# The second norm's result turned in 32x32 blocks by VectorE and moved by DMA, the low-rank part one step later

## What is computed

```
x = _layernorm(x + attn(x, wq, wk, wv, wo))        # 32 heads of 32, grouped keys, causal
x = _layernorm(x + xattn(x, ctx, weight))          # three-tap convolution over the sequence's rows
x = _layernorm(x + ffn(x, A, B, Wr, br))

ffn:    router_logits = x @ Wr.T + br              # 8 experts
        scores = 8 * softmax(router_logits)
        low = x @ A.T                              # 8 experts of rank 16: 128 values a row
        out = 2 * sum over experts and rank of low * scores * B
```

## Time and profile before

| | us |
|---|---|
| runs, median (lowest to highest) | 1471.19 (1468.21 to 1471.94) |
| profiled execution, its own time | 1470.48 |
| its span, first to last instruction | 1468.6 |
| first stage, to about | 816 |
| second stage, steady steps | 850 to 1426 |
| tail of the second stage | 1427 to 1468.6 |

### The profile page before, as it was taken

The page is one execution under the profiler, slowest core; times in us unless marked ns, Lnnn a source line. Parts: engine busy times, 40 slices in busy tenths (PEclk is TensorE's granted clock), DMA queues, the critical chain, the costliest instruction groups (busy, mean ns, idle before and its releaser), DMA issues. The chain is left out here.

```text
span 1468.6 us, 32393 instructions
## 1 busy us (share of the span) xinstructions
PE 1368.0 (93%) x8288; PEld 1058.0 (72%) x8288; DVE 1092.8 (74%) x3965; ACT 930.5 (63%) x3258; POOL 984.2 (67%) x936
## 2 busy tenths in 40 slices
PE   6899999999999999999996699999999999999994
PEld 4667676676676676766764488888888888888873
DVE  5767777777777677777776468877888888778875
ACT  5777777787878777777877255545555555545543
POOL 3667676667667676666666377777777777777763
PEclk9999999999999999999998799999999999999997
DMA  6345444444445344444447767667766666767651
GB/s 224 113 117 147 120 139 130 123 143 116 142 116 143 116 144 119 139 130 123 145 138 208 186 158 159 161 162 170 168 150 159 163 165 156 160 164 171 156 116 44
DMA packets 108861, 213.03 MB, mean 145 GB/s; under 512 B 26640, under 2 KB 32272, under 8 KB 108816
## 3 DMA queue, kind: packets, MB, share of 16 engines
q1 hardware_dynamic: 108816, 212.51, 54.1%
HBM read 131.83 MB, written 34.47 MB: 113 GB/s over the span
## 5 line engine op out<-in xcount | busy, mean ns | idle before, releaser
L432 PE MATMUL wo_ps<-weights,halves 128*128 128x512 f32 x2304 | 572.5, 399 | 12.1 <-DVE weights L610 12.0
L432 PEld LDWEIGHTS wo_ps<-weights,halves 128*128 128x128 f32 x2304 | 422.6, 189 | 129.5 <-issue 34.4
L693 ACT ACTIVATE pexp<-sm,smin 128x128 f32<-128x128 f32 x1024 | 398.3, 392 | 175.9 <-DVE smin L561 175.8
L1040 PE MATMUL wo_ps<-weights,halves 128*128 128x512 f32 x1488 | 400.6, 402 | 2.0 <-DVE yz L1143 2.0
L812 POOL TENSOR_TENSOR pn<-pexp,prec 128x512 f32<-128x512 f32 x256 | 268.8, 1050 | 196.2 <-DVE prec L568 196.2
L1393 POOL TENSOR_TENSOR prods<-prod,prods 128x512 fp32r<-128x512 f32 x192 | 260.3, 1364 | 133.8 <-ACT prods L1287 128.9
L1040 PEld LDWEIGHTS wo_ps<-weights,halves 128*128 128x128 f32 x1488 | 273.0, 190 | 61.0 <-issue 3.7
L561 DVE CUSTOM_DVE_ANT_0 sm<-s_ps,mask_t 128x128 f32<-128x128 f32 x1024 | 231.9, 282 | 67.0 <-PE s_ps L462 62.3
L1287 ACT CAST prods<-prod 128x512 fp32r<-128x512 f32 x192 | 118.8, 621 | 165.8 <-DVE prod L1177 129.3
L1177 DVE TENSOR_TENSOR prod<-att,x 128x512 f32<-128x512 f32 x192 | 186.1, 985 | 13.9 <-DMA att<-sim_scratch 11.1
L693 ACT ACTIVATION_READ_ACCUMULATOR pexp<-sm,smin 128x1 f32 x1024 | 193.5, 189 | 0.0
(11 more groups left out here) (99 smaller groups left out, 1661.1 us busy)
## 6 DMA issues: line engine op xcount, KB each, us to landing
att<-sim_scratch SPq DMA_DIRECT2D x192, 252.0 KB
pt<-blocks SPq DMA_DIRECT2D x640, 64.0 KB, 2.0
ctx_t<-in_ctx SPq DMA_DIRECT2D x32, 576.0 KB, 4.7
raw<-in_xT SPq DMA_DIRECT2D x32, 512.0 KB, 3.6
raw<-ot_scratch SPq DMA_DIRECT2D x32, 512.0 KB, 6.8
xn<-in_x SPq DMA_DIRECT2D x32, 512.0 KB, 7.5
out<-late SPq DMA_DIRECT2D x32, 512.0 KB, 6.3
ot_scratch<-ot SPq DMA_DIRECT2D x63, 256.0 KB, 2.1
```

What stands on the lines that cost most here:

```text
L432: mm = pe.matmul(qkv_ps[(par + g) % 2][:], xs[:, par, xl, k], w_sb[:, wl, g, k], start=(k == 0 and n == 0), stop=(k == KT - 1 and n == 2))
L693: ins = nc.scalar.activation(pexp[:, c % 2, i * P:(i + 1) * P], sm[:, c % 2, i * P:(i + 1) * P], ACT.Exp, bias=smin[:, c % 2, i:i + 1], sc ...
L1040: mm = pe.matmul(wo_ps[n][:], os_t[:, par, ol, k], wo_sb[:, wl, k, n * BANK:(n + 1) * BANK], start=(k == 0 and m == 0), stop=(k == KT - 1 ...
```

## The change

x2 is no longer turned by PE, except for the last two tokens (30 and 31, whose work lies in the tail). Instead DVE turns it in 32x32 blocks with one instruction (`block_x2`) into a new tile `blocks`, whose layout is [partition, block of rows, row, k], so that its writes lie KT = 8 numbers apart. SP then moves the 4x4 blocks with sixteen DMAs (`move_x2`), each 32 partitions by 256 numbers (32 KB), into `xt`, whose layout is now [partition, row, k]: `reduce_rank` reads its stationary operand `xt[:, :, k]` with a step of 8 numbers. `reduce_rank`, `route`, `gates` and `gate_low` now work on token z = t-3, one step later than before, and `turn_low`, `low_lt` and `expand` follow in the same step. The store of the output is one step later too. `prods` and `lt` move into the place of weights no longer used.

```
     def later_weights(weights):
...
+            hi[:, rest:rest + PB * 2 * BANK].rearrange("p (m l n) -> p m l n", m=PB, l=2),
+            lo[:, rest + 2 * TAPS * P:rest + 2 * TAPS * P + 2 * S].rearrange("p (l s) -> p l s", l=2))
...
-    xt = sb("xt", [P, KT, S])
+    blocks = sb("x2_blocks", [P, QB, SB, KT])
+    xt = sb("xt", [P, S, KT])
...
-    LAST = B + 2
-    LEAD, TAIL = 6, 5
+    LAST = B + 3
+    LEAD, TAIL = 6, 6
+    MOVES = 16 * QB * QB
...
+        def move_x2(t):
+            wait(sp, low_done, after(t - 1, 1, 1))
+            wait(sp, x2_blocked, after(t, 1, 1))
+            for b in range(QB):
+                for q in range(QB):
+                    sp.dma_start(xt[q * SB:(q + 1) * SB, b * SB:(b + 1) * SB], blocks[b * SB:(b + 1) * SB, q]
+                                 ).then_inc(xt_in, 16)
...
+            if valid(t - 4):
+                wait(sp, normed[2], after(t - 4, 1, 1))
+                sp.dma_start(out[t - 4], res[:, par]).then_inc(stored[par], 16)
             if valid(t) and not at_step(t, 0):
                 load_att(t, 0)
-            if valid(t - 3):
-                wait(sp, normed[2], after(t - 3, 1, 1))
-                sp.dma_start(out[t - 3], res[:, 1 - par]).then_inc(stored[1 - par], 16)
+            if valid(t - 2) and not at_step(t, B) and not at_step(t, B + 1):
+                move_x2(t - 2)
             if valid(t) and not at_step(t, 0):
                 load_att(t, 1)
...
         def reduce_rank(t):
-            wait(pe, xt_in, after(t, 2, 2))
+            if at_step(t, 0):
+                pe.wait_ge(consts_in, 48)
+            if at_step(t, B - 2) or at_step(t, B - 1):
+                pe.wait_ge(xt_copied, 2 * (t - B + 3))
+            else:
+                wait(pe, xt_in, after(t, MOVES, MOVES))
+                wait(pe, added[2], after(t - 1, 2, 1))
             for k in range(KT):
-                mm = pe.matmul(ffn_place(t)[0][:, 0:LOWW], xt[:, k], wa_t[:, k * LOWW:(k + 1) * LOWW],
+                mm = pe.matmul(ffn_place(t)[0][:, 0:LOWW], xt[:, :, k], wa_t[:, k * LOWW:(k + 1) * LOWW],
                                start=(k == 0), stop=(k == KT - 1))
             mm.then_inc(low_done, 1)
...
                 if valid(z):
-                    if s == 1:
+                    if s == 3:
+                        reduce_rank(z)
+                    if s == 10:
                         turn_low(z)
-                    if s == 3:
+                    if s == 13:
                         expand(z)
-                if valid(f):
-                    if s in (11, 12):
-                        turn_x2(f, par, s - 11)
-                    if s == 14:
-                        reduce_rank(f)
...
         convolve(B - 2, 4)
-        turn_low(B - 3)
+        reduce_rank(B - 3)
         convolve(B - 2, 5)
-        expand(B - 3)
...
+        def block_x2(t, par):
+            wait(dve, normed[1], after(t, 1, 1))
+            wait(dve, xt_in, after(t, MOVES, 0))
+            dve.transpose(blocks[:].rearrange("p q s k -> p q k s"),
+                          x2[:, par].rearrange("p (k q d) -> p q k d", k=KT, q=QB)).then_inc(x2_blocked, 1)
```

More of the change, by code:

```diff
@@ L100, in later_weights @@
 def later_weights(weights):
-    lo = weights[:, NG * KT * BANK:2 * NG * KT * BANK]
+    hi, lo = (weights[:, part * NG * KT * BANK:(part + 1) * NG * KT * BANK] for part in range(2))
     both = weights[:].rearrange("p (l m) -> p l m", l=2)
@@ L1055, in turn_x2 @@
         def turn_x2(t, par, n):
-            if at_step(t, 0) and n == 0:
-                pe.wait_ge(consts_in, 48)
-            wait(pe, normed[1], after(t, 1, 1))
-            if at_step(t, B - 2):
+            pe.wait_ge(normed[1], t + 1)
+            if t == B - 2:
                 pe.wait_ge(added[0], 2 * (B - 1) + n + 1)
             else:
-                last = t - 2 if at_step(t, B - 1) else t - 1
-                wait(pe, added[2], after(last, 2, n + 1))
+                pe.wait_ge(added[2], 2 * (t - 2) + n + 1)
             for k in range(NJ):
@@ L1078, in turn_low @@
             wait(pe, gated_done, after(t, 1, 1))
+            if not at_step(t, B - 2) and not at_step(t, B - 1):
+                wait(pe, added[2], after(t - 1, 2, 2))
             pe.transpose(ffn_place(t)[1][:, 0:S], gated[:], id_t[:]).then_inc(low_turned, 1)
@@ L1218, in step @@
                 average(f, 1)
+            if valid(z):
+                route(z)
             if valid(c):
                 multiply(c, 1 - par, 1)
+            if valid(z):
+                gate_low(z)
+            if valid(c):
+                multiply(c, 1 - par, 2)
+            if valid(t):
+                add(t, par, 0, 0)
+                count(t, 0, 0)
+            if valid(z):
+                low_lt(z)
+            if valid(f):
+                block_x2(f, par)
+            if valid(c):
+                multiply(c, 1 - par, 3)
+                multiply(c, 1 - par, 4)
+            if valid(z):
+                add(z, 1 - par, 2, 0)
+                add(z, 1 - par, 2, 1)
+            if valid(c):
+                add(c, 1 - par, 1, 0)
+                count(c, 1, 0)
             if valid(z):
@@ L1225, in step @@
             if valid(c):
[L1226 to L1237 removed]
                 multiply(c, 1 - par, 5)
[L1239 to L1242 removed]
+        steps(dve, step, 0, B - 1, LEAD, TAIL - 4)
         def finish(t):
@@ L1257, in _ @@
         average(B - 2, 1)
-        for m in range(PB):
-            multiply(B - 1, 1, m)
+        multiply(B - 1, 1, 0)
+        route(B - 3)
+        multiply(B - 1, 1, 1)
+        gate_low(B - 3)
+        multiply(B - 1, 1, 2)
+        low_lt(B - 3)
+        multiply(B - 1, 1, 3)
         finish(B - 3)
-        for m in range(PB, UNITS):
-            multiply(B - 1, 1, m)
+        multiply(B - 1, 1, 4)
+        multiply(B - 1, 1, 5)
         add(B - 1, 1, 1, 0)
@@ L1297, in normalise2 @@
             wait(act, shifted[1], after(t, 1, 1))
+            wait(act, added[2], after(t - 2, 2, 2))
             nc.scalar.activation(x2[:, par], yz[:, 1], ACT.Identity, bias=shift[1][:],
@@ L1301, in copy_x2 @@
         def copy_x2(t, n):
[L1302 to L1305 removed]
+            act.wait_ge(x2_turned, 2 * (t - B + 2) + n + 1)
+            act.wait_ge(low_done, t)
+            nc.scalar.copy(xt[:, :, n * NJ:(n + 1) * NJ].rearrange("p s k -> p k s"),
+                           ffn_place(t)[n][:].rearrange("p (k s) -> p k s", k=NJ)).then_inc(xt_copied, 1)
         def gates(t):
@@ L1340, in step @@
             if valid(z):
-                normalise3(z, 1 - par)
-            if valid(f):
-                copy_x2(f, 0)
-            if valid(c):
-                high_prod(c, 3)
-            if valid(f):
-                copy_x2(f, 1)
-            if valid(c):
-                high_prod(c, 4)
-            if valid(f):
-                gates(f)
-            if valid(c):
-                high_prod(c, 5)
-        steps(act, step, 0, B - 1, LEAD, TAIL - 3)
+                high_lt(z)
+            if valid(c):
+                for m in range(PB, UNITS):
+                    high_prod(c, m)
+            if valid(z):
+                normalise3(z, 1 - par)
+        steps(act, step, 0, B - 1, LEAD, TAIL - 4)
+        normalise1(B - 1, 1)
+        high_prod(B - 1, 0)
+        gates(B - 3)
+        high_prod(B - 1, 1)
+        normalise2(B - 2, 0)
         high_lt(B - 3)
-        normalise1(B - 1, 1)
-        normalise2(B - 2, 0)
-        for m in range(UNITS):
+        for m in range(2, UNITS):
             high_prod(B - 1, m)
@@ L1420, in step @@
             if valid(c):
-                for m in range(3, UNITS):
-                    low_prod(c, m)
-        steps(pool, step, 0, B - 1, LEAD, TAIL - 3)
+                low_prod(c, 3)
+                low_prod(c, 4)
+            if valid(z):
+                invert_root(z, 2)
+            if valid(c):
+                low_prod(c, 5)
+        steps(pool, step, 0, B - 1, LEAD, TAIL - 4)
         invert_root(B - 1, 0)
```

51 lines of the change are left out of this document (15 added, 36 removed).

## The result

| | before | after |
|---|---|---|
| runs, median (lowest to highest), us | 1471.42 (1468.21 to 1471.94) | 1660.08 (1658.57 to 1661.06) |
| profiled execution, its own time | 1470.48 | 1659.12 |
| its span | 1468.6 | 1657.3 |
| mean granted TensorE clock | 0.982 | 0.936 |

The changed kernel takes 1.1286 times as long, interval [1.1267, 1.1306]. The forecast was 1567, with a range to 1655: the direction is right, the size is not. The measured time lies outside the range, 5 us above its end.

A forecast was written before the change was run, and what follows sets the result against it. PE was taken to bound the kernel at 19.48 us a step; the change makes a longer loop through DVE and SP's moves. Start 866.1, 28 rounds of 22.6, 15.8, then tail 41.8 + 8.4 give span 1564.9, time 1567, range 1505 to 1655.

The forecast's parts named there:

- The rounds: Low-rank product to low-rank product, 28 times: chain through PE, DVE and SP of 22.2 us, plus 0.4 for clock, 22.6.
- what follows from token 28's product on: End of kernel: 15.8 us left of step 31, then the tail's 41.8 plus 8.4 for the last tokens' later work.
- The bound, the moved wait and the moves: PE would idle 3.6 us a round before the low-rank product, awaiting sixteen SP moves of 11.35 us to last landing.
- DVE's part of the chain without the turn: Second norm, router and gate, third product, next token's statistics and half of lt on DVE; 7.42 us including a turn of 1.38.
- DVE's own round: DVE's work of 18.0 us a step plus a 2.2 us hole before the first product: 20.2, above the present 19.48.
- The block turn: DVE's new turn of 1024 numbers a partition: 1.38 us, twice the row for 512; low end 1.2, high end 2.8.
- The product: PE's low-rank product reading xt, priced at its present 1.85 us in the round.
- rival B: Strided access doubles the block turn (1.4 more) and low-rank product (1.85 more): round 25.4, time 1652; chance 0.23.
- The clock term: PE behind its new pause: lower clock could add 2.4 us a round; 0.4 was charged.
- One in six: Assumed share of PE's new pauses followed by the lower clock, giving 0.4 us a round.
- Rival A: DVE's own round of 20.2 us binds if moves are issued faster, from 0.49 apart: time 1500; chance 0.14.
- Rival C: PE stays the bound and time falls by 26 us to 1445, needing moves landed within 7.8 us; chance 0.05.

The follow-up runs named there:

- the kernel that doesn't wait: Changed kernel with doubled xt, its low-rank product using moves issued a step earlier, and read and write unstepped: 1464.99 us, 0.9963 of the kernel before.
- wide moves: Changed kernel with eight moves of 512 numbers a partition instead of sixteen of 256, both accesses still stepped: 1503.73 us, 1.0228 of the kernel before.
- pause filled: Changed kernel with read and write unstepped, plus twelve unused matmuls just ahead of the low-rank product: 1559.03 us, against 1602.91 without them.
- the last kernel: Changed kernel with k ahead of the row in both tiles, SP issuing eleven moves and ACT five, behind its high halves of products 3 and 4: 1497.55 us.
- short runs on two queues: Changed kernel with k ahead of the row in both tiles (128-byte runs), SP issuing eleven moves and ACT five ahead of its high halves: 1501.35 us.

## Why the forecast was right in its mechanism and wrong in its size

From 1564.9 to 1657.3 the span is 92.4 off. The rounds carry 28 x (25.53 - 22.6) = 82; the first product is at 866.01 (866.1 forecast), and what follows from token 28's product on takes 76.4 instead of 66.0. Three products in its chain of waits, 4.2, 4.2 and 3.7 where 1.85 stood, are 6.6 of these 10.4; the rest was not taken apart.

The 2.93 that a round is too long by can be split with the stepped product's 4.09 behind a wait at full clock: the product + 2.24, the block turn + 0.83, the clock + 0.16, DVE's other work - 0.31, together 2.92. Over 28 rounds that is 63 + 23 + 4 - 9 = 81 of the 82. **The step that failed is the price of the two stepped accesses, above all 1.85 for the product.**

- **The bound, the moved wait and the moves: right.** The sixteen moves take 15 x 0.634 + 1.88 = 11.39 from first issue to last landing; forecast 11.35. PE waits for them in every round, DVE for ACT 2.3 and for the convolution piece. Line 306's ten moves were the right row for moves of half the size. (Their 6.23 us span nine distances and one issue, so that the row says 0.627 rather than 0.623.)
- **DVE's part of the chain without the turn: 0.3 too long.** From the convolution piece to the turn it is 5.73, forecast 7.42 - 1.38 = 6.04. The third product takes 0.69, not 0.9: the product's mean fell to 706 ns from 985. In the steady part before, 72 of 124 products ran for most of their time beside an instruction of POOL of over 0.9 us and took 1.25 us in the mean, and those with little or none beside them 0.68; in after none ran so. The two go together; no experiment changed that alone. DVE's own round, put at 20.2, is 18.93, of which 1.1 comes from cheaper products: one takes 831 ns in the mean of 1000 to 1400 in the kernel that doesn't wait, against 1009 before, six times a round.
- **The block turn: mis-sized.** 1.38 forecast, 2.21 measured, + 0.83 a round or 23 us. The unstepped turn takes 1.23; the stepped write was the part that no row of before showed, and I took the value nearest to the row without a step. The bound of 2.8 held it.
- **The product: failed, and it is the largest miss.** 1.85 forecast. The stepped read makes it 3.70 at full clock (wide moves, no wait), which was rival B's value, and 4.09 at full clock behind a wait. In after it is 4.10 to 4.23, always behind a wait. Of the + 2.24, 1.97 is the step and 0.27 the start behind a wait, which the plain product shows too (2.12 for 1.85).
- **The clock term: wrong in its reasoning, near in its size by luck.** "One in six" should have been all. PE's part of the chain, product, projection and convolution piece, takes 5.5 and 6.6 in turn, mean 6.04. At full clock the same three take 4.09 + 0.69 + 0.70 = 5.48 behind a wait in the kernel with wide moves, so the clock costs 0.56 a round where 0.4 was forecast. It is so little only because the stepped read leaves the product nothing to lose: with both accesses unstepped, as the forecast priced them, the clock costs 1.45 (pause filled against not), and the forecast would have been 28 x 1.05 = 29 us short by it. I had one pause of 4.30 with the clock low behind it, and gave the new pause of 3.6 a sixth of that by its shorter length. Pauses of 3.4 were already followed by the low clock in nearly all rounds.
- **Rival B: right in its mechanism.** Its price for the product came true (3.70), that for the turn about half (+ 0.83 for + 1.4), and its round, 25.4, is 0.1 short of the measured 25.53, its time, 1652, 8 us. That it came so near is in part luck: it charged too much for the turn, and nothing for the clock and for the start behind a wait. The Trainium skill (Advanced Engine Details and Errata, section SBUF Cachelines) has the penalty for accesses that each touch another line, and the runs agree: 1.23 to 2.21 for DVE's write, 1.85 to 3.70 for PE's weight read. The page's rule spoke for B and I gave B 0.23.
- **Rival A** (DVE binds) is excluded for after by DVE's waits. It became true only in the kernel that doesn't wait for its moves. **Rival C** (PE stays the bound) is excluded; it needed the moves off the chain, and then the time is 1465 to 1505, not 1445, since DVE or the stepped read takes over.

The forecast's own arithmetic is tested by the kernel with both accesses unstepped and the pause filled: 1559.03 measured against 1564.9 + 1.9 - 28 x 0.4 = 1556 without the clock term. So the structure of the sum stands. What failed are the prices of the two operations whose stepped access no row showed: both were put in as if the step were free, and both lie in the one chain that sets the round.

What stays open: why the rounds of the last kernel differ among themselves (19.1 to 22.3). The clock accounts for some of the long ones. Its moves also land later in some, and no run tells whether the other transfers or the short runs are the reason.

## What to carry to other kernels

A change that takes work off the bound engine but sends its input round three others makes a new loop: sum that loop, with every DMA issue in it at the issuing engine's pitch (0.63 us each here, whatever the bytes), and compare it with the bound engine's own work. If the loop is longer, the bound engine pauses once a round. Behind pauses of TensorE of 3.4 us and more, once a round, the clock fell in nearly every round here; so charge it in each, but only to operations that nothing else holds up already. And where the new layout makes an engine step 32 bytes between float32 numbers, take twice the unstepped time for it until a run shows otherwise.

## What the runs showed of the hardware

- Stepping 32 bytes costs nearly the factor of two on both sides: DVE's block turn of 1024 numbers takes 2.21 instead of 1.23 when its write steps, PE's sixteen float32 matmuls of 136 columns 3.70 instead of 1.85 when the weight read steps, both at full clock. The mean weight load is 334 ns against 190.
- A product whose weight read steps hardly feels the clock. After has two in its tail that PE doesn't wait for; its timeline, and the windows in them:

```profile
1631.87 3.89 PE L1090 MATMUL wo_ps<-wa_t,xt 128*128 128x136 f32 x16
1640.14 3.87 PE L1090 MATMUL ffn_ps<-wa_t,xt 128*128 128x136 f32 x16
```

```profile
1634.00:1635.00 1.00, 1.00 (x6) 1.00 (x6) 0.15 (x2) 0.00 (x0) 0.69 (x2) 0.50 0.00 0
1641.00:1642.00 1.00, 1.00 (x6) 1.00 (x5) 0.97 (x3) 0.00 (x0) 0.00 (x0) 1.00 0.00 0
```

  3.89 with most of it at half the clock and 3.87 at the full one; behind a wait 4.22 and 4.09. The plain product goes from 2.12 to 3.99 behind a wait. The four times fit two limits of which the larger one counts, so that taking away either alone brings little.
- Pauses of 3.4 to 4.4 us of PE once a round were followed by a granted clock of 0.50 in nearly every round, pauses of 0.75 in none; in the last kernel, with pauses of 0.5 to 2.7 in front of the product, the clock was low in it in four of 28 rounds. Twelve needless matmuls in the pause brought 44 us.
- Moves from SBUF to SBUF in runs of 128 bytes are little dearer than in runs of 1 KB: landing 2.0 instead of 1.9, pitch 0.66 instead of 0.633, 20 us in all. The Trainium skill (DMA: Bandwidth & Descriptors, section Why small descriptors are slow (HBM only)) says that transfers within SBUF don't pay for small descriptors, and for the landing on one queue the trace agrees. It doesn't for the DMA engines' own time: a packet of 128 bytes took 14 ns in the mean and one of 1 KB 62 to 65, so the same bytes keep the engines busy 1.7 times as long. With short runs on two queues the DMA share is 0.89 and the median landing of SP's moves 3.8 instead of 2.0.
- ACT issues a DMA in about the time that SP does (median 0.61 and 0.59), and its timeline has no other instruction while it issues; nor while it waits for what the first issue needs.
